# An xLSTM attention and routed feed-forward block: the output combined in expert order instead of in token order

## The chip, the cores and the metric

The kernel runs on one core of one Trainium2 chip. The time is that of the device, in microseconds, of one execution. The kernel before took 240.93 us, the median of 3 runs (239.75 to 241.77).

## The reference, cut to what matters

```python
x = L0_attn_x                          # (16, 256, 128) float32, 4096 tokens
xn = _layernorm(x)
s = _L0_attn_ref(xn, ...)              # 4 heads of 32; each head's row is normalised
                                       # to mean 0 and variance 1, then times (1 + ln_w)
# feed-forward: each token goes to one of 8 experts (argmax of the router)
top1 = argmax(softmax(xn @ router_w + router_b))
for i in range(8):
    a, g = split(xn @ w1[i] + b1[i])   # 128 -> 2 x 512
    y = (a * sigmoid(g)) @ w2[i] + b2[i]
    out = out + where(top1 == i, y, 0)
g = silu(out)
x = x + s * g                          # what is returned
```

So each token's row of the output is its own `x`, plus its attention row `s` times the silu of its expert's row.

## The kernel before, in words

The 4096 tokens are 32 tiles of 128 rows. **First**, up to about 52 us, the rows are normalised and transposed, and the router and gate projections are made; for each token its place in expert order is worked out (`pos`): the tokens of an expert stand together, padded to whole blocks of 128 rows, which makes `NBLK` = 39 blocks in `NCH` = 13 chunks of three. **Then** attention runs over the 16 sequences, up to about 107 us, while POOL scatters the 32 tiles of normalised rows `xw` (each row with its token's number behind it) to `xs_dram` in expert order, with one indirect DMA a tile (line 443). Attention leaves its raw head rows in `u_all`.

**Then** the expert blocks run. In iteration j, PE transposes the rows of block j+1 (`rowsT`, line 1131), makes the hidden products of block j (`hidden`, line 1195: the gate half first, then the other half) and the down products of block j-1 (`down`, line 1204). ACT in iteration j copies the transposed rows out (`evac_xs`, line 606), copies one half of the next block's weights (`copy_w`, line 600), takes the sigmoid of the gate (`gate`, line 612), and the sigmoid for the silu of block j-2 (line 656). DVE copies the other half of the next block's weights (`copy_w`, line 851), multiplies by the gate (`product`, line 976), adds the bias (`add_bias`, line 984) and finishes the silu of block j-2 (`silu`, line 992). PE waits for both weight halves of a block (`s_wc`, `s_wv`), the second half of `hidden` only for DVE's, and `down(j)` waits for `product(j)`. Weights are held three deep, so `copy_w(j+1)` in iteration j waits for `hidden(j-2)`.

Between these pieces DVE does the attention's normalisation in small pieces: `step(normals)` issues the next instruction of the generator `normalise`, three times in an iteration, each after a wait that the one before is done. There are four groups of eight tiles and 25 steps a group: two squares (line 918), two sums (line 920), nineteen small ones on 128x32 elements, and two products with the coefficient (line 934). POOL multiplies each finished group by gamma (line 457) back into `u_all`, between its other work.

POOL scatters each finished silu block to `y_dram` in token order, one indirect DMA a block (line 449); rows that are padding have an index out of bounds and are dropped. SP loads the chunks of sorted rows four deep (line 335), and, after the sixth, reloads `x` (line 341).

**Last**, when all 39 scatters have landed, SP reads `y_dram` back in 8 pieces (line 347); DVE multiplies each piece by the attention rows (line 963); `x` is added by PE in four pieces (lines 1261 and 1265, evacuated by ACT, line 660), by POOL in three (line 465) and by DVE in one (line 968); and SP stores each piece (line 356).

Of the kernel before, what the change touches and what calls it, by code (L numbers as in the profile page):

```python
# [5 lines left out]
F32 = mybir.dt.float32  # L6
# [7 lines left out]
P = 128  # L14


def mlstm_moe_block(nc, x, wq, wk, wv, wi, bi, wf, bf, ln_w, router_w, router_b, w1, b1, w2, b2, out):
# [18 lines left out]
    NX = 4  # L36
# [11 lines left out]
    GROUPS = [(0, 4), (4, 4), (8, 4), (12, 4)]  # L48
    NPC = 8
    TP = T // NPC  # L50
    POOL_PIECES = (2, 4, 6)
    PE_PIECES = (0, 1, 3, 5)
# [4 lines left out]
    GT = 8  # L57
# [7 lines left out]
    y_dram = nc.dram_tensor("y_tokens", (NTOK, D), F32).ap()  # L65
    x_t = x.rearrange("b (k p) d -> p (b k) d", p=P)
    y_t = y_dram.rearrange("(t p) d -> p t d", p=P)
    out_t = out.rearrange("b (k p) d -> p (b k) d", p=P)

    ctx = ExitStack()  # L70
    with ctx:
# [10 lines left out]
        yg = xn  # L82
        xnT = sb("xnT", [P, NTOK])
        u_all = sb("u_all", [P, T, NH, DA])
# [72 lines left out]
        q_all = x_sb[:, :, :].rearrange("p t d -> p (t d)")  # L157

# [12 lines left out]
        sqs = [cflat[:, i * GT * D:(i + 1) * GT * D].rearrange("p (t h d) -> p t h d", t=GT, h=NH) for i in range(2)]  # L171
# [6 lines left out]
        ys_sb = ffn[:, 0:2 * CH * D].rearrange("p (i n d) -> p i n d", i=2, n=CH)  # L178
# [58 lines left out]
        s_yst = [sem(f"s_yst{i}") for i in range(NX)]  # L237
        s_yg = [sem(f"s_yg{i}") for i in range(NPC)]
# [3 lines left out]
        s_fin = sem("s_fin")  # L242
        s_finp = sem("s_finp")
        s_fina = sem("s_fina")
        s_sum = sem("s_sum")
        s_gam = sem("s_gam")
        s_prod = sem("s_prod")
        s_out = sem("s_out")
# [48 lines left out]
        s_xr = sem("s_xr")  # L297
        s_gamma = sem("s_gamma")

        NSMALL = 7  # L300
        block = ctx.enter_context(nc.Block())
# [3 lines left out]
        def _(sp):  # L305
# [22 lines left out]

            sp.wait_ge(s_sub, 5)
            sp.wait_ge(s_scat, 16 * T)  # L330
            for c in range(NCH):
                if c >= NX:
                    sp.wait_ge(s_xsp, (c - NX + 1) * CH)
                    sp.wait_ge(s_idx, c - NX + 1)
                sp.dma_start(xs_sb[:, c % NX, :, :],
                             xs_dram[c * CH * P:(c + 1) * CH * P, :].rearrange("(n p) d -> p n d", p=P)).then_inc(s_xs[c % NX], 16)
                if c == NX + 1:
# [10 lines left out]
            for g in range(NPC):  # L348
                ts = slice(g * TP, (g + 1) * TP)
                if g in POOL_PIECES:  # L350
                    sp.wait_ge(s_finp, POOL_PIECES.index(g) + 1)
                elif g in PE_PIECES:
                    sp.wait_ge(s_fina, PE_PIECES.index(g) + 1)
                else:
                    sp.wait_ge(s_fin, len([i for i in range(g + 1) if i not in POOL_PIECES + PE_PIECES]))
                sp.dma_start(out_t[:, ts, :], yg[:, ts, :]).then_inc(s_out, 16)
            sp.wait_ge(s_out, 16 * NPC)
# [3 lines left out]
        def _(pool):  # L361
# [84 lines left out]
            for j in range(NBLK):  # L446
                pool.wait_ge(s_ye, j + 1)
                pool.wait_ge(s_idx, j // CH + 1)
                pool.indirect_dma_start(y_dram, bass.IndirectOffsetOnAxis(ap=idx[:, j:j + 1], axis=0),  # L449
                    ys_sb[:, j // CH % 2, j % CH, :], None, bounds_check=NTOK - 1, oob_is_err=False).then_inc(s_yst[j // CH % NX], 16)  # L450

                if j in GAMMA_AT:
                    g = GAMMA_AT.index(j)
                    b0, nb = GROUPS[g]
                    pool.wait_ge(s_norm, NSTEPS * (g + 1))
                    pool.wait_ge(s_gamma, 1)
                    pool.tensor_tensor(u_all[:, 2 * b0:2 * (b0 + nb), :, 0:DH], sqs[g % 2],
                                       gamma[:, :].rearrange("p (h d) -> p h d", h=NH).unsqueeze(1).to_broadcast([P, GT, NH, DH]),
                                       ALU.mult).then_inc(s_gam, 1)

            for g in POOL_PIECES:
                y = yg[:, g * TP:(g + 1) * TP, :]
                pool.wait_ge(s_xr, 16 * NPC)
                pool.wait_ge(s_prod, g + 1)
                pool.tensor_tensor(y, y, x_sb[:, g * TP:(g + 1) * TP, :], ALU.add).then_inc(s_finp, 1)
# [3 lines left out]
        def _(act):  # L469
# [187 lines left out]

            for i, g in enumerate(PE_PIECES):
                act.wait_ge(s_sum, i + 1)
# [629 lines left out]
```

## Time and profile before

| | |
|---|---|
| median of 3 runs | 240.93 us (239.75 to 241.77) |
| the profiled execution, its own time | 240.99 us |
| its span in the profile | 239.2 us |
| mean granted TensorE clock | 0.975 |
| PE busy | 209.1 us (87%) |
| DVE busy | 181.8 us (76%) |
| ACT busy | 136.5 us (57%) |
| POOL busy | 100.0 us (42%) |
| moved by DMA | 29.30 MB |

The shares of busy time are averages over stages that have different limits; where the time goes is read from the chain of work that ended last and from the order in time of single instructions. The device time is 1.8 us more than the span of this execution.

### The profile page before, as it was taken

Reading aid. Unit: us, or ns where it says so; the run is one execution under the profiler, and the core shown is the slowest. Engines: PE = TensorE matmul, PEld = TensorE weight load, DVE = VectorE, ACT = ScalarE, POOL = GpSimd, SP = SyncE. Lnnn points to the kernel's source line nnn. Section 1 sums busy time; section 2 is a strip of 40 time slices with the busy share of each in tenths; the row PEclk is TensorE's granted clock in tenths of the full one; section 3 lists DMA queues with packets and bytes.
Section 4 is the critical chain, followed back from the end, with each engine's and each line's share of the span. In section 5 each row is a group of like instructions: output and inputs, shape, how many; then the busy total and the mean of one; then the engine's idle time right before and its main releaser. Section 6 shows DMA issues by size and latency. Waiting matters only on the chain.

```text
span 239.2 us, 6066 instructions
## 1 busy us (share of the span) xinstructions
PE 209.1 (87%) x1824; PEld 170.8 (71%) x1832; DVE 181.8 (76%) x505; ACT 136.5 (57%) x313; POOL 100.0 (42%) x128
## 2 busy tenths in 40 slices
PE   0688879689999999979999999999999999999650
PEld 0568744335555555559999999999999999986310
DVE  6997378299989986648777988898889789671490
ACT  0276756779788796754555555555555655540110
POOL 7553200027777776000333364425533464366150
PEclk9988999999999999999999999999999999999975
DMA  6999999501441111401097021102101000000994
GB/s 175 266 419 418 282 299 394 221 3 46 146 137 53 49 53 59 115 21 33 15 261 204 26 58 52 55 22 62 44 30 50 28 25 25 26 11 13 251 315 137
DMA packets 29730, 29.30 MB, mean 122 GB/s; under 512 B 3295, under 2 KB 24807, under 8 KB 29697
## 3 DMA queue, kind: packets, MB, share of 16 engines
q1 hardware_dynamic: 26258, 24.59, 33.0%
q0 software_dynamic: 2272, 4.22, 5.4%
q8 instruction: 16, 0.26, 0.5%
q10 hardware_dynamic: 1168, 0.10, 0.4%
q14 instruction: 16, 0.13, 0.2%
HBM read 20.01 MB, written 9.34 MB: 123 GB/s over the span
## 4 chain that ended last, share of the span: by engine, by line
PE 67%; DVE 11%; issue 6%; ACT 5%; DMA 5%; DVEq 1%; SPq 1%; POOL 1%; ACTq 0%; POOLq 0%
PE bank L1195 13%; PE head_bank L1195 13%; PE bank L1204 12%; PE head_bank L1159 5%; PE bank L1169 5%; PE bank L1149 4%; PE head_bank L1052 4%; PE bank L1180 3%; PE bank L1148 3%; DMA xw<-y_tokens 2%; DVE stats L696 2%; PE bank L1037 2%; PE bank L1082 2%; DVE cm L859 2%; PE head_bank L1131 1%
## 5 line engine op out<-in xcount | busy, mean ns | idle before, releaser
L449 POOL DMA_INDIRECT y_tokens<-ffn,idx x39 | 39.2, 1004 | 76.3 <-DVE ffn L992 74.0
L443 POOL DMA_INDIRECT xs_sorted<-xw,pos x32 | 33.0, 1031 | 36.3 <-DVE pos L831 26.9
L1204 PE MATMUL bank<-w_sb,dm 128*128 x312 | 41.3, 275 | 0.5 <-DVE dm L976 0.5
L1195 PE MATMUL bank<-xsT,wc 128*128 128x128 f32 x320 | 39.3, 276 | 0.1
L1204 PEld LDWEIGHTS bank<-w_sb,dm 128*128 128x128 f32 x312 | 38.0, 192 | 0.7 <-issue 0.7
L1195 PEld LDWEIGHTS bank<-xsT,wc 128*128 128x128 f32 x320 | 37.4, 192 | 0.5 <-DVE wc L851 0.3
L1195 PE MATMUL head_bank<-xsT,wc 128*128 128x128 f32 x304 | 37.0, 275 | 0.0
L1195 PEld LDWEIGHTS head_bank<-xsT,wc 128*128 128x128 f32 x304 | 35.4, 192 | 0.0
L859 DVE TENSOR_TENSOR cm<-dm,head_bank 128x1024 f32<-128x1024 f32 (+1 forms) x32 | 29.0, 948 | 6.3 <-ACT dm L586 3.5
L600 ACT ACTIVATE wc<-w_sb 128x512 f32 x39 | 24.6, 630 | 14.3 <-issue 14.3
L586 ACT ACTIVATE dm<-bank 128x512 f32<-128x512 f32 x48 | 26.9, 594 | 4.5 <-PE bank L1149 3.5
L606 ACT ACTIVATE xsT<-head_bank 127x128 f32<-127x128 f32 x38 | 10.5, 277 | 27.8 <-PE head_bank L1131 27.8
L851 DVE COPY wc<-w_sb 128x512 f32 x39 | 16.6, 425 | 10.3 <-issue 9.0
L1149 PE MATMUL bank<-right,left 128*128 128x512 bf16 x48 | 15.7, 379 | 2.6 <-ACT x_sb L535 1.0
L1159 PEld LDWEIGHTS head_bank<-x_sb,xnT 32*128 32x128 f32 x256 | 11.7, 184 | 8.0 <-issue 7.7
L976 DVE TENSOR_TENSOR dm<-bank,dm 128x512 f32<-128x512 f32 x20 | 13.6, 681 | 3.7 <-ACT dm L612 2.0
L1159 PE MATMUL head_bank<-x_sb,xnT 32*128 32x256 f32 (+1 forms) x256 | 15.0, 347 | 0.5 <-DVE cm L859 0.4
L976 DVE TENSOR_TENSOR dm<-head_bank,dm 128x512 f32<-128x512 f32 x19 | 13.0, 684 | 2.3 <-ACT dm L612 2.3
L984 DVE TENSOR_TENSOR ffn<-bank,b_sb 128x128 f32<-128x128 f32 x39 | 11.2, 287 | 4.4 <-PE bank L1204 2.1
L656 ACT ACTIVATE ffn<-ffn 128x128 f32<-128x128 f32 x39 | 11.8, 302 | 4.9 <-DVE ffn L984 4.9
L1169 PE MATMUL bank<-cm,u_all 128*32 128x256 f32 (+1 forms) x256 | 13.7, 332 | 0.0
L612 ACT ACTIVATE dm<-bank 128x512 f32<-128x512 f32 x20 | 11.6, 581 | 2.9 <-PE bank L1195 2.9
(199 smaller groups left out, 352.0 us busy)
## 6 DMA issues: line engine op xcount, KB each, us to landing
x_sb<-in_L_attn_x SPq DMA_DIRECT2D x16, 256.0 KB, 5.1
w_sb<-in_L_ffn_w SPq DMA_DIRECT2D x8, 512.0 KB, 8.2
wc<-in_L_ffn_w SPq DMA_DIRECT2D x5, 512.0 KB, 17.1
xs_sb<-xs_sorted SPq DMA_DIRECT2D x13, 193.5 KB, 2.8
xs_sorted<-b_sb SPq DMA_DIRECT2D x1, 2048.0 KB, 17.3
xw<-y_tokens SPq DMA_DIRECT2D x8, 256.0 KB, 4.6
out_x<-xw SPq DMA_DIRECT2D x8, 256.0 KB, 3.6
y_tokens<-ffn,idx POOLq DMA_INDIRECT x39, 2.3
```

The lines of the kernel that those rows point to most:

```text
L443: pool.indirect_dma_start(xs_dram, bass.IndirectOffsetOnAxis(ap=pos[:, t:t + 1], axis=0), xw[:, t, :], None).then_inc(s_scat, 16)
L449: pool.indirect_dma_start(y_dram, bass.IndirectOffsetOnAxis(ap=idx[:, j:j + 1], axis=0), ys_sb[:, j // CH % 2, j % CH, :], None, bounds_ch ...
L586: act.activation(dm[:, b % 2, :, m, :], bank[(3 * b + m) % 2][:, :].rearrange("p (h t) -> p h t", h=NH), ACT.Exp).then_inc(s_dm, 1)
L600: act.activation(wc[:, j % 3, HID:H2], w1_sb[:, bass.ds(e, 1), HID:H2], ACT.Copy).then_inc(s_wc, 1)
L851: dve.tensor_copy(wc[:, j % 3, 0:HID], w1_sb[:, bass.ds(e, 1), 0:HID]).then_inc(s_wv, 1)
L859: dve.tensor_tensor(cm[:, b % 2, :, m0:m1, :], dm[:, b % 2, :, m0:m1, :], head_bank[:, :, m0 * P:m1 * P].rearrange("p h (m t) -> p h m t", ...
L976: dve.tensor_tensor(uT[:, j % 2, :, :].rearrange(flat), bank[2 * (j % 2)][:, :], sg[:, j % 2, :, :].rearrange(flat), ALU.mult).then_inc(s_ ...
L1149: pe.matmul(bank[n % 2][:, :], left[:, b % 4, s0:s0 + P], right[:, :, j, t0:t0 + P], start=(m == 1), stop=True).then_inc(s_ld, 1)
L1159: last = pe.matmul(head_bank[:, h, 2 * k * P:(2 + k) * P], xnT[hs, b * S + k * P:b * S + (k + 1) * P], q_all[hs, b * S + k * P:(b + 1) * S ...
L1169: last = pe.matmul(bank[6][h * DH:(h + 1) * DH, k * P:S], u_all[:, 2 * b + k, h, 0:DH], cm[:, b % 2, h, 2 * k:2 + k, :].rearrange("p m t - ...
L1195: last = pe.matmul(bank[2 * (j % 2) + k][:, c * P:(c + 1) * P], wc[:, j % 3, m:m + P], xsT[:, j % 2, :], start=True, stop=True)
L1204: last = pe.matmul(bank[6 + j % 2][:, 0:D], uT[:, j % 2, c, :], w2_sb[:, bass.ds(e * (HC * D) + c * D, D)], start=(c == 0), stop=(c == HC ...
```

## The change

`y_dram`, the read back in token order and the whole last stage are taken out. In their place the attention rows are brought into expert order, and the combination is made there.

- The normalisation has two groups of sixteen tiles, each in four quarters of 128x512 elements. The squares are made by ACT (`squares(i)`, in iterations 0 to 7, between `evac_xs` and `copy_w`); the result goes into `sall`, which lies in the place of `xnT`. The sums wait for them (`s_sq`). The gamma of the first group is multiplied by POOL in two instructions of 128x1024, after steps 25 and 27; that of the second group by DVE, after each quarter.
- POOL scatters the 32 tiles of finished attention rows into `ss_dram` in expert order, the first sixteen from `hidden(9)` on, the other sixteen from `hidden(18)` on. SP fills `ss_dram` with zeros and copies `x` to the output, DRAM to DRAM, both right after its load of chunk 3. After its load of chunk 10, SP waits for all 32 scatters and loads ten chunks of `ss`; the other three follow as slots come free.
- The silu blocks stay in `yall`, ten chunks deep, in the place of `xw`. `combine(c)` multiplies a whole chunk (128x384) by its `ss` rows, in iterations 27 to 38 for chunks 0 to 11; the three blocks of chunk 12 are multiplied singly in `silu`.
- POOL then scatters the 39 blocks to the output rows with an adding indirect DMA (`compute_op=ALU.add`), the first when `combine(0)` is done. The kernel ends when these have landed.

```diff
-    GROUPS = [(0, 4), (4, 4), (8, 4), (12, 4)]
-    NSTEPS = 25
-    GAMMA_AT = (9, 18, 27, 34)
+    GROUPS = [(0, 8), (8, 8)]
+    NQ = 4
+    SMALL_STEPS = NQ + 19
+    NSTEPS = (SMALL_STEPS + NQ, SMALL_STEPS + 2 * NQ)
+    NSLOT = 10
+    COMBINE_AT = [27 + c for c in range(NCH - 1)]
...
@@ SP @@
+                if c == NX - 1:
+                    blanks = zeros[:, :]
+                    sp.dma_start(ss_of_p[:, 0:full * S].rearrange("p (n c) -> p n c", n=full),
+                                 blanks.unsqueeze(1).to_broadcast([P, full, S])).then_inc(s_ssf, 16)
+                    sp.dma_start(ss_of_p[:, full * S:NBLK * D], blanks[:, 0:NBLK * D - full * S]).then_inc(s_ssf, 16)
+                    sp.dma_start(out_rows, x.rearrange("b s d -> (b s) d")).then_inc(s_pre, 16)
+                if c == NCH - 3:
+                    sp.wait_ge(s_ss, 16 * T)
                     sp.wait_ge(s_sc, B)
-                    for g in range(NPC):
-                        ts = slice(g * TP, (g + 1) * TP)
-                        sp.dma_start(x_sb[:, ts, :], x_t[:, ts, :]).then_inc(s_xr, 16)
-            for i in range(NX):
-                sp.wait_ge(s_yst[i], 16 * CH * len(range(i, NCH, NX)))
-            for g in range(NPC):
-                ts = slice(g * TP, (g + 1) * TP)
-                sp.dma_start(yg[:, ts, :], y_t[:, ts, :]).then_inc(s_yg[g], 16)
...
+                    for i in range(NSLOT):
+                        load_s(i)
+            for i in range(NSLOT, NCH):
+                sp.wait_ge(s_cb, i - NSLOT + 1)
+                load_s(i)
@@ POOL @@
-            for j in range(NBLK):
-                pool.wait_ge(s_ye, j + 1)
-                pool.wait_ge(s_idx, j // CH + 1)
-                pool.indirect_dma_start(y_dram, bass.IndirectOffsetOnAxis(ap=idx[:, j:j + 1], axis=0),
-                    ys_sb[:, j // CH % 2, j % CH, :], None, bounds_check=NTOK - 1, oob_is_err=False).then_inc(s_yst[j // CH % NX], 16)
...
+            def scatter_s(t):
+                pool.indirect_dma_start(ss_dram, bass.IndirectOffsetOnAxis(ap=pos[:, t:t + 1], axis=0),
+                                        sall[:, t, :, :].rearrange("p h d -> p (h d)"), None).then_inc(s_ss, 16)
+            pool.wait_ge(s_gamma, 1)
+            for i in range(2):
+                rows = sall[:, i * 2 * QT:(i + 1) * 2 * QT, :, :]
+                pool.wait_ge(s_norm, SMALL_STEPS + 2 * (i + 1))
+                pool.tensor_tensor(rows, rows, gamma_hd(2 * QT), ALU.mult).then_inc(s_gam, 1)
+            pool.wait_ge(s_ssf, 32)
+            for t in range(GT):
+                pool.wait_ge(s_gam, t // (2 * QT) + 1)
+                pool.wait_ge(s_h, 10 + t // 2)
+                scatter_s(t)
+            for t in range(GT, T):
+                pool.wait_ge(s_norm, NSTEPS[0] + SMALL_STEPS + 2 * ((t - GT) // QT + 1))
+                pool.wait_ge(s_h, 19 + (t - GT) // 3)
+                scatter_s(t)
+            pool.wait_ge(s_pre, 16)
+            for c in range(NCH):
+                for n in range(CH):
+                    j = CH * c + n
+                    if c < NCH - 1:
+                        pool.wait_ge(s_cb, c + 1)
+                    else:
+                        pool.wait_ge(s_ye, j + 1)
+                    pool.wait_ge(s_idx, c + 1)
+                    pool.indirect_dma_start(out_rows, bass.IndirectOffsetOnAxis(ap=idx[:, j:j + 1], axis=0),
+                                            yall[:, c % NSLOT, n, :], None, bounds_check=NTOK - 1, oob_is_err=False,
+                                            compute_op=ALU.add).then_inc(s_ost[min(c, NCH - NSLOT)], 16)
@@ ACT @@
+            def squares(i):
+                ts = slice(i * QT, (i + 1) * QT)
+                act.wait_ge(s_sc, B)
+                act.wait_ge(s_oe, (i + 1) * QT // 2)
+                act.activation(sall[:, ts, :, :], u_all[:, ts, :, 0:DH], ACT.Square).then_inc(s_sq, 1)
             for j in range(NBLK + 2):
                 if j + 1 < NBLK:
                     evac_xs(j + 1)
+                if j < 2 * NQ:
+                    squares(j)
                 if 1 <= j < NBLK - 1:
                     copy_w(j + 1)
@@ DVE @@
+                for i, (a, b) in enumerate(quarters):
+                    dve.wait_ge(s_sq, NQ * g + i + 1)
+                    yield dve.tensor_reduce(ssum[:, a * NH:b * NH], sall[:, t0 + a:t0 + b, :, :], AX.X, ALU.add)
...
+                for a, b in quarters:
+                    rows = sall[:, t0 + a:t0 + b, :, :]
+                    yield dve.tensor_tensor(rows, uv[:, a:b, :, :],
                                             coef[:, a * NH:b * NH].rearrange("p (t h) -> p t h", h=NH).unsqueeze(3).to_broadcast([P, b - a, NH, DH]),
                                             ALU.mult)
+                    if g == 1:
+                        dve.wait_ge(s_gamma, 1)
+                        yield dve.tensor_tensor(rows, rows, gamma_hd(QT), ALU.mult)
...
+            def combine(c):
+                y = yall[:, c % NSLOT, :, :]
+                dve.wait_ge(s_ye, CH * (c + 1))
+                dve.wait_ge(s_ssl[c], 16)
+                dve.tensor_tensor(y, y, ss[:, c % NSLOT, :, :], ALU.mult).then_inc(s_cb, 1)
...
                 if j >= 2:
                     silu(j - 2)
+                if j in COMBINE_AT:
+                    combine(COMBINE_AT.index(j))
                 step(normals)
-            while step(normals):
-                pass
-            finish()
```

The last stage's instructions on PE, ACT and POOL go with `finish()`.

## Rows read from the trace of the kernel before

**Rows 1.** The page, busy time by engine: busy us, share, instructions.
```profile
PE 209.1 (87%) x1824; PEld 170.8 (71%) x1832; DVE 181.8 (76%) x505; ACT 136.5 (57%) x313; POOL 100.0 (42%) x128
```
**Rows 2.** Chain of work that ended last: start us, us, engine, tile, line.
```profile
211.69 1.80 PE bank L1195 x16
...
217.60 0.98 POOL y_tokens L449
218.89 2.10 DMA y_tokens<-ffn,idx
```
**Rows 3.** Order in time, PE: start us, us, line, operation [idle before].
```profile
110.86 1.95 PE L1195 MATMUL bank<-xsT,wc 128*128 128x128 f32 x16
...
135.96 1.95 PE L1195 MATMUL head_bank<-xsT,wc 128*128 128x128 f32 x16
...
144.33 2.31 PE L1195 MATMUL bank<-xsT,wc 128*128 128x128 f32 x16
...
180.95 1.95 PE L1195 MATMUL head_bank<-xsT,wc 128*128 128x128 f32 x16
...
211.52 1.95 PE L1195 MATMUL bank<-xsT,wc 128*128 128x128 f32 x16
```
**Rows 4.** Order in time, POOL.
```profile
91.30 0.96 POOL L443 DMA_INDIRECT xs_sorted<-xw,pos  x1 [0.31 <-issue]
92.56 0.96 POOL L443 DMA_INDIRECT xs_sorted<-xw,pos  x1 [0.30 <-issue]
...
141.77 2.39 POOL L457 TENSOR_TENSOR u_all<-cm,gamma 128x1024 f32<-128x1024 f32 x1
...
186.02 0.98 POOL L449 DMA_INDIRECT y_tokens<-ffn,idx  x1 [1.25 <-DVE ffn L992]
...
217.60 0.98 POOL L449 DMA_INDIRECT y_tokens<-ffn,idx  x1 [0.30 <-issue]
218.89 0.98 POOL L449 DMA_INDIRECT y_tokens<-ffn,idx  x1 [0.31 <-issue]
```
**Rows 5.** Line 449's instructions: duration ns min/median/max, and the way to landing.
```profile
L449 POOL DMA_INDIRECT y_tokens<-ffn,idx x39: 982/984/1147, 115.1 to 218.9; - x39
DMA to landing us min/median/max: 2.1/2.3/4.3
```
**Rows 6.** Order in time, DVE.
```profile
112.20 0.43 DVE L851 COPY wc<-w_sb 128x512 f32 x1
...
131.85 0.42 DVE L851 COPY wc<-w_sb 128x512 f32 x1
132.19 0.68 DVE L918 TENSOR_TENSOR cm<-u_all 128x512 f32<-128x512 f32 x1
...
134.98 0.41 DVE L851 COPY wc<-w_sb 128x512 f32 x1
...
141.54 2.68 DVE L930 TENSOR_SCALAR veps<-ssum 128x32 f32<-128x32 f32 x1
...
184.97 0.28 DVE L992 TENSOR_TENSOR ffn<-ffn 128x128 f32<-128x128 f32 x1
```
**Rows 7.** Order in time, ACT, the row copy of iteration 3.
```profile
113.85 0.28 ACT L606 ACTIVATE xsT<-head_bank 127x128 f32<-127x128 f32 x1 [0.82 <-PE head_bank L1131]
```
**Rows 8.** Groups of instructions by line, keeping shapes apart: busy us, mean ns | idle before.
```profile
L600 ACT ACTIVATE wc<-w_sb 128x512 f32 x39 | 24.6, 630 | 14.3 <-issue 14.3
L920 DVE TENSOR_REDUCE ssum<-cm 128x16 f32<-128x512 f32 x8 | 5.4, 675 | 0.0
```
**Rows 9.** SP's queue in order of time, and the page's issues with us to landing.
```profile
119.81 6.14 SPq L341 DMA_DIRECT2D x_sb<-in_L_attn_x  x8
x_sb<-in_L_attn_x SPq DMA_DIRECT2D x16, 256.0 KB, 5.1
xs_sb<-xs_sorted SPq DMA_DIRECT2D x13, 193.5 KB, 2.8
```
**Rows 10.** Stretch with one scatter an iteration: us, busy (x) of PE, PEld, DVE, ACT, POOL, PEclk, DMA share, GB/s.
```profile
186.00:213.00 27.00, 27.00 (x245) 27.00 (x244) 21.20 (x60) 14.93 (x37) 14.08 (x12) 1.00 0.07 24
```

More of the change, by code:

```diff
@@ L64, in mlstm_moe_block @@
     xs_dram = nc.dram_tensor("xs_sorted", (NBLK * P, DW), F32).ap()
-    y_dram = nc.dram_tensor("y_tokens", (NTOK, D), F32).ap()
+    ss_dram = nc.dram_tensor("s_sorted", (NBLK * P, D), F32).ap()
     x_t = x.rearrange("b (k p) d -> p (b k) d", p=P)
-    y_t = y_dram.rearrange("(t p) d -> p t d", p=P)
-    out_t = out.rearrange("b (k p) d -> p (b k) d", p=P)
+    out_rows = out.rearrange("b s d -> (b s) d")
     ctx = ExitStack()
@@ L236, in mlstm_moe_block @@
         s_ye = sem("s_ye")
-        s_yst = [sem(f"s_yst{i}") for i in range(NX)]
-        s_yg = [sem(f"s_yg{i}") for i in range(NPC)]
+        s_ssl = [sem(f"s_ssl{c}") for c in range(NCH)]
+        s_ost = [sem(f"s_ost{i}") for i in range(NCH - NSLOT + 1)]
+        s_ss = sem("s_ss")
+        s_ssf = sem("s_ssf")
+        s_pre = sem("s_pre")
+        s_cb = sem("s_cb")
+        s_sq = sem("s_sq")
+        s_mix = sem("s_mix")
         s_norm = sem("s_norm")
@@ L296, in mlstm_moe_block, with gamma_hd @@
         s_xone = sem("s_xone")
-        s_xr = sem("s_xr")
         s_gamma = sem("s_gamma")
         NSMALL = 7
+        def gamma_hd(n):
+            return gamma[:, :].rearrange("p (h d) -> p h d", h=NH).unsqueeze(1).to_broadcast([P, n, NH, DH])
         block = ctx.enter_context(nc.Block())
@@ L336, in _ @@
                              xs_dram[c * CH * P:(c + 1) * CH * P, :].rearrange("(n p) d -> p n d", p=P)).then_inc(s_xs[c % NX], 16)
-                if c == NX + 1:
-                    sp.wait_ge(s_sc, B)
-                    for g in range(NPC):
-                        ts = slice(g * TP, (g + 1) * TP)
-                        sp.dma_start(x_sb[:, ts, :], x_t[:, ts, :]).then_inc(s_xr, 16)
-            for i in range(NX):
-                sp.wait_ge(s_yst[i], 16 * CH * len(range(i, NCH, NX)))
-            for g in range(NPC):
-                ts = slice(g * TP, (g + 1) * TP)
-                sp.dma_start(yg[:, ts, :], y_t[:, ts, :]).then_inc(s_yg[g], 16)
[L348 to L357, printed above, removed]
+                if c == NX - 1:
[6 more added lines that the diff above has]
+                    sp.wait_ge(s_ss, 16 * T)
+                    sp.wait_ge(s_sc, B)
+                    for i in range(NSLOT):
[3 more added lines that the diff above has]
+                load_s(i)
+            for i in range(NCH - NSLOT + 1):
+                sp.wait_ge(s_ost[i], 16 * CH * (1 if i < NCH - NSLOT else NSLOT))
         @block.gpsimd
@@ L656, in _ @@
                     act.activation(sy[:, j % 2, :], yb[:, j % 2, :], ACT.Sigmoid).then_inc(s_sy, 1)
-            for i, g in enumerate(PE_PIECES):
-                act.wait_ge(s_sum, i + 1)
-                act.activation(yg[:, g * TP:(g + 1) * TP, :], bank[i][:, :].rearrange("p (t d) -> p t d", d=D), ACT.Copy).then_inc(s_fina, 1)
         @block.vector
@@ L911, in normalise @@
                 dve.wait_ge(s_oe, b0 + nb)
[L912 to L920 removed]
+                t0 = 2 * b0
+                quarters = [(i * nt // NQ, (i + 1) * nt // NQ) for i in range(NQ)]
+                for i, (a, b) in enumerate(quarters):
+                    dve.wait_ge(s_sq, NQ * g + i + 1)
+                    yield dve.tensor_reduce(ssum[:, a * NH:b * NH], sall[:, t0 + a:t0 + b, :, :], AX.X, ALU.add)
+                yield dve.scalar_tensor_tensor(den[:, 0:n].rearrange("p (t h) -> p t h", h=NH), rs, -1.0, rs, ALU.mult, ALU.max)
                 d4 = den[:, 0:n].rearrange("p (b k h) -> p b k h", k=2, h=NH)
[L923 removed]
                 yield dve.tensor_tensor(d4, d4, tm[:, :, :].rearrange("p k (h b) -> p b k h", h=NH)[:, b0:b0 + nb, :, :], ALU.max)
@@ L953, in _ @@
             norms = [0]
-            def finish():
-                for g in range(NPC):
-                    ts = slice(g * TP, (g + 1) * TP)
-                    y = yg[:, ts, :]
-                    hd = "p t (h d) -> p t h d"
-                    dve.wait_ge(s_yg[g], 16)
-                    dve.wait_ge(s_gam, len(GROUPS))
-                    dve.tensor_tensor(y.rearrange(hd, h=NH), y.rearrange(hd, h=NH), u_all[:, ts, :, 0:DH],
-                                      ALU.mult).then_inc(s_prod, 1)
-                    if g not in POOL_PIECES + PE_PIECES:
-                        dve.wait_ge(s_prod, g + 1)
-                        dve.wait_ge(s_xr, 16 * NPC)
-                        dve.tensor_tensor(y, y, x_sb[:, ts, :], ALU.add).then_inc(s_fin, 1)
             def product(j):
```

75 lines of the change are left out of this document (24 added, 51 removed).

## The prediction, made before the result was known

> **What bounds the kernel now.** I read the page's busy shares first, to see that no engine fills the span: PE is at 87%, POOL at 42% [rows 1]. Then the chain of waits. From about 108 us on it is one PE link after another up to the last hidden products at 211.69; then come POOL's last scatters and a landing of 2.10 from 218.89 [rows 2]; behind it stand the read back, the last products and the stores. Then PE in order of time: hidden(2) starts at 110.86 and hidden(38) at 211.52, 36 iterations at 2.80 us [rows 3]. Only once in that stretch is a hidden longer than 1.95 (2.31, at 144.33), so PE sets the pace, and DVE, ACT and POOL are late by less than PE forgives. The last stage, from the landing at 221.0 to the end at 239.2, is 18.2 us. This is what the change takes out; the question is what is then last.
>
> **The queue of adding scatters.** Before, POOL had one scatter an iteration, started about 0.77 us after its silu, as the one of block 25: silu from 184.97 to 185.25 [rows 6], scatter at 186.02 [rows 4]. After, all 39 output scatters stand behind combine(0), which DVE makes in iteration 27, right behind silu(25), and they stand in one queue. Back to back, POOL starts a scatter every 1.29 us at the end of the kernel and every 1.26 beside attention: 0.96 to 0.98 busy and 0.30 of issue each [rows 4]. Three a chunk are 3.9 us, where chunks come every 2.80. So POOL falls behind from the first chunk, and the end is that of a queue:
> - combine(0), 128x384 with both inputs in SBUF, lies between 0.28 for 128x128 and 0.68 for 128x512 [rows 6]; 0.55 by interpolation. It ends at 185.7, and the first adding scatter starts at 186.5.
> - 38 intervals. Their ends: 1.26, and 1.45, which is the longest scatter seen, 1.147, plus 0.30 [rows 4, 5]. I take 1.30, since the median is 0.984 and some beside a busy DVE are longer: 49.4 us, last start at 235.9.
> - Landing 2.1 to 4.3, median 2.3 [rows 5]: 238.2, and 0.1 to the span's end: **238.3**.
>
> That stands against a span of 239.2. Of the 18.2 us removed 17.3 come back as a queue on POOL, before any delay upstream. No row shows a scatter that adds. From below I give it the plain price (nothing in the trace excludes that it costs no more), from above the longest duration and the longest landing: 38 x 0.15 + 2.0 = 7.7 us more. The nearest row is the plain scatter to DRAM of the same 128 rows, so I take its price and keep the upper end for the range.
>
> **What delays iteration 27.** The chain starts at a fixed iteration, so each microsecond that PE or DVE loses before it moves the end by one.
> - *Squares on ACT, sums on DVE.* Each square is 128x512 from SBUF to SBUF, as the weight copy at 0.63; ACT, at 57%, has room for eight. But DVE's steps outrun them. The third step of iteration 1 is the sum of quarter 3, and its square stands on ACT behind the row copy of iteration 3, which ends at 114.13 [rows 7]. Square to 114.8, sum (0.675, [rows 8]) to 115.4, 0.3 of issue, then copy_w(3) to 116.1, which before ended at 112.63 [rows 6]. hidden(3) starts at 113.66 (110.86 + 2.80) and wants it for its second half at 114.6. PE loses **1.5 us**; bounds 0 and 2.
> - *Gamma on POOL.* Before, DVE's step of 128x32 at 141.54 took 2.68 us, ending with POOL's 128x1024 product (141.77, 2.39): DVE's instruction was held [rows 4, 6]. Before, such products were eight iterations apart and PE lost 0.4 at the worst. After, there are two, after steps 25 and 27, in iterations 8 and 9, where DVE is fullest: it goes from copy at 131.85 to copy at 134.98 without a gap, 3.13 us for a pace of 2.80 [rows 6]. Two holds are 3.8 to 4.8 us; copy_w(11) has 1.5 us to spare (ends 135.39, wanted at 136.86, 0.9 after 135.96). That leaves 2.3 to 3.3; less the 0.4 lost before, and some of a hold falling on the sums, I take **2.2**; bounds 0 and 4.
>
> The Trainium skill (SBUF — State Buffer, Who interferes with whom) says that the port pair is held for the whole instruction by whoever issues first, and that `tensor_reduce` never contends. By that rule the four sums of group 1 next to the products run on, and copies and two-input products wait; the trace agrees as far as it goes (2.68 beside 2.39). If sums were held as well, the stall would be nearer the upper bound, 4.
>
> - *DVE, the rest.* Removed: eight squares and eight products become twelve others of like size, so the number of heavy steps hardly falls; the second group's eight products in iterations 17 to 19 go at 3.13 an iteration, 1.0 us late over three, inside the 1.5 to spare. The twelve combines meet iterations without steps. Nothing.
> - *POOL before the queue.* 32 scatters of attention rows. The first sixteen start at about 141 and end by 161; the others start with hidden(18) done, at about 161, and 16 x 1.26 = 20.2 bring them to 182, landed by 185. SP then issues ten loads, 2.8 us to landing [rows 9]: chunk 0 is there at about 189, when combine(0) comes at 185.7 + 3.7 = 189.4. Hidden, but by little. If it failed, it would cost 1 to 3 us. Loads of chunks 11 and 12 wait behind this on SP, and are wanted only four iterations later.
> - *SP after chunk 3.* The fill (2.5 MB) and the copy of x (2 MB read and written) go ahead of chunk 4. Eight loads of 256 KB were issued in 6.14 and landed 5.1 later, 2 MB in 11 us [rows 9]. So the fill is 14 and the copy 11 to 22: from 99.5, done by 125 to 136; chunk 4 is wanted in iteration 11, at about 137. Hidden, with 1 us at the worst. Taken out: the reload of x and the read back; the former cost PE nothing.
>
> **Sum.** 238.3 + 1.5 + 2.2 = 242.0 span. The profiled execution was 240.99 for 239.2, 1.8 more, and 0.06 above the median: **243.8 us**. A difference of 1% (238.5 to 243.3) is about what a measurement of this kernel can tell from none.
>
> **Rivals.**
> - *The queue as computed, PE's stalls forgiven.* DVE's lateness has been absorbed nearly wholly in the trace (one hidden at 2.31 against four gamma products). Against: never two holds in two iterations, never a step that waits for ACT. Time: 238.3 to 239.8 and 1.8, **240.1 to 241.6**, no change. 20%.
> - *An adding scatter is dearer than a plain one*, in POOL's work or because its landing holds the next. Each 0.1 us an interval is 3.8. At 1.45 and a landing of 4.3, with the stalls, **251.5**, or more. For: every row must be read, added to and written back. Against: with a plain scatter every 2.8 us the DMA engines are busy 0.07 of the time [rows 10], and POOL need not wait for a landing. 13%.
> - *Faster: the intervals are shorter than 1.29.* The place is the 0.30 of issue between scatters. Without it 38 x 0.30 = 11.4 are saved: span 230.6 with the stalls, **232.4**. With stalls, 238.5 is passed only below 1.16 an interval (5.3 us over 38); without stalls at 1.26, the rate beside attention. For: the new waits are met long before, so that nothing has to come in from another engine. Against: 0.30 to 0.31 before every back-to-back scatter [rows 4]. 8%.
> - The Trainium skill (SBUF — State Buffer, the trap of DVE blocking a DMA) has POOL locked out of writing descriptors while DVE copies from SBUF to SBUF, 0.62 us growing to 3.1. As a mechanism of this kernel it would be one hold for each of the eleven copies beside the queue. The rows show scatters beside such copies at 1.147 at most, so 11 x 0.16 = 1.8 us, **245.6**; it lies inside the case I forecast, a third of whose chance it has.
>
> **How the numbers follow.** The forecast case, queue and stalls, has 59% and spans 241.5 to 249. The range leaves out the rest of the fast rival and half of the dear one: 239.5 to 251. Slower by over 1% (above 243.3): two thirds of 59% and the 13%, 0.53. Within 1%: a third of 59% and 18% of the second, 0.38. Faster: 0.09.
>
> **What would show it.** Right: POOL issues 39 scatters to the output without a gap, 1.3 us apart, from about 190 to 240, with PE idle after 218; hidden(3) is some 3.4 us long; a copy or product of DVE beside each POOL product is 2 us or more; hidden(27) starts about 3.7 us later than at 180.95 [rows 3]. Wrong: intervals above 1.4; hidden(27) before 182; a combine that waits for a load; scatters that wait for DVE, which would mean that POOL keeps up.

## The result, and the profile after

The changed kernel takes **273.66 us** (median of 4 runs, 272.50 to 274.71) against 240.80 us for the one before, measured beside it: 1.1365 times, with a 95% interval of 1.1295 to 1.1434. I had forecast 243.8 in a range of 239.5 to 251.0: the sign was right, the size far off. The profiled execution took 272.50 us for a span of 270.6.

The page of the changed kernel, its busy times, the row of the software queue (packets, MB, share) and its POOL groups (line 477 is the output scatter, line 447 that of the normalised rows, line 451 that of the attention rows; line 458, further down, is POOL's product with gamma):

```profile
span 270.6 us, 6060 instructions
PE 198.2 (73%) x1798; PEld 164.3 (61%) x1798; DVE 172.0 (64%) x469; ACT 137.9 (51%) x317; POOL 145.7 (54%) x155
...
q0 software_dynamic: 7664, 6.32, 13.3%
...
L477 POOL DMA_INDIRECT out_x<-xw,idx x39 | 61.6, 1579 | 18.1 <-issue 10.4
L447 POOL DMA_INDIRECT xs_sorted<-xw,pos x32 | 33.0, 1030 | 36.4 <-DVE pos L849 26.9
...
L451 POOL DMA_INDIRECT s_sorted<-xnT,pos x32 | 32.0, 1000 | 11.8 <-issue 7.5
```

POOL's busy time grew from 100.0 to 145.7 us [rows 1], and not by number alone: the two plain kinds of scatter take 1.00 and 1.03 us, the adding one 1.58. The chain of waits names it too: from 209 us on it is one POOL link behind another. Here are POOL in order of time at the start of the queue and at its end, and then the summary of line 477 and line 70, where the program closes (EVENT_SEMAPHORE and DRAIN are the sequencers' own; for them too the columns are ns and start):

```profile
182.61 0.96 POOL L451 DMA_INDIRECT s_sorted<-xnT,pos  x1 [0.30 <-issue]
190.04 1.61 POOL L477 DMA_INDIRECT out_x<-xw,idx  x1 [6.47 <-DVE xw L1008]
191.96 1.58 POOL L477 DMA_INDIRECT out_x<-xw,idx  x1 [0.30 <-issue]
...
261.65 1.55 POOL L477 DMA_INDIRECT out_x<-xw,idx  x1 [0.30 <-issue]
```
```profile
L477 POOL DMA_INDIRECT out_x<-xw,idx x39: 1554/1554/1926, 190.0 to 261.7; - x39
...
L70 POOLq DRAIN  x1: 29477/29477/29477, 240.9 to 240.9; - x1
...
L70 SPq COMPARE_BRANCH  x1: 37/37/37, 264.5 to 264.5; - x1
...
L70 SPq EVENT_SEMAPHORE  x1: 17/17/17, 270.6 to 270.6; - x1
```

Three things are to be seen. The queue is there from 190.04 to 261.65 with nothing but 0.30 us between two scatters, which the view calls issue (the engine waits for nothing that the profile shows): 38 intervals in 71.61 us, **1.884 us** each, where plain scatters stood 1.29 apart [rows 4]. Its start is where I put it (190.2). And the program does not end with the last landing: SP is past its waits at 264.5, but POOL's closing DRAIN runs until 240.91 + 29.48 = 270.4, and the closing events of the other engines stand behind it. (The DRAIN is entered at 240.91, when twelve scatters are still to start, so its length says little; what counts is its end, 7.2 us behind the end of the last scatter.)

On PE the two losses upstream can be read directly. PE in order of time, the iterations around them, and hidden(27):

```profile
107.65 1.95 PE L1210 MATMUL head_bank<-xsT,wc 128*128 128x128 f32 x16
...
113.23 1.06 PE L1210 MATMUL head_bank<-xsT,wc 128*128 128x128 f32 x8
115.57 1.16 PE L1210 MATMUL head_bank<-xsT,wc 128*128 128x128 f32 x8 [1.28 <-DVE wc L869]
...
117.56 1.95 PE L1210 MATMUL bank<-xsT,wc 128*128 128x128 f32 x16
...
136.91 1.15 PE L1219 MATMUL bank<-w_sb,dm 128*128 x8 [0.66 <-DVE dm L978]
...
138.01 1.06 PE L1210 MATMUL head_bank<-xsT,wc 128*128 128x128 f32 x8
140.93 1.16 PE L1210 MATMUL head_bank<-xsT,wc 128*128 128x128 f32 x8 [1.86 <-DVE wc L869]
...
185.18 1.95 PE L1210 MATMUL head_bank<-xsT,wc 128*128 128x128 f32 x16
```

The second half of hidden(3) waits 1.28 us for DVE's weight copy, down(9) 0.66 for its product, and the second half of hidden(11) 1.86 for the copy again. What a wait costs is read from the starts, since it is more than the idle time shown: hidden(4) starts 4.33 us behind hidden(3) (117.56 and 113.23), 1.54 over the pace of 2.79; hidden(12) at 143.30 starts 9.00 behind hidden(10) at 134.30, 3.42 over two iterations. DVE in order of time shows why: first the sums that wait for squares (line 934, behind ACT's line 663), then two instructions of 2.86 and 2.45 us. The last two lines are POOL's, its two products with gamma beside them:

```profile
111.54 0.69 DVE L934 TENSOR_REDUCE ssum<-xnT 128x16 f32<-128x512 f32 x1 [1.12 <-ACT xnT L663]
...
114.33 0.69 DVE L934 TENSOR_REDUCE ssum<-xnT 128x16 f32<-128x512 f32 x1 [1.68 <-ACT xnT L663]
115.09 0.43 DVE L869 COPY wc<-w_sb 128x512 f32 x1
...
132.97 0.42 DVE L869 COPY wc<-w_sb 128x512 f32 x1
133.31 2.86 DVE L948 TENSOR_TENSOR xnT<-u_all,coef 128x512 f32<-128x512 f32 x1
...
137.49 2.45 DVE L996 TENSOR_TENSOR xw<-ffn 128x128 f32<-128x128 f32 x1
139.87 0.67 DVE L934 TENSOR_REDUCE ssum<-xnT 128x16 f32<-128x512 f32 x1
```
```profile
133.21 2.41 POOL L458 TENSOR_TENSOR xnT<-xnT,gamma 128x1024 f32<-128x1024 f32 x1 [39.06 <-DVE xnT L948]
137.44 2.35 POOL L458 TENSOR_TENSOR xnT<-xnT,gamma 128x1024 f32<-128x1024 f32 x1 [1.83 <-DVE xnT L948]
```

The runs differ by up to 4 us in when the expert blocks begin (hidden(1) at 107.65 to 111.56; e8 apart), so below I compare from the start of hidden(1) on. In the changed kernel that is 107.65, hidden(27) comes **77.53 us** behind it, the queue 4.86 behind that, and the end 162.95 behind hidden(1). Before: hidden(1) at 108.07, hidden(27) at 180.95 [rows 3], 72.88 behind.

### The profile page after: what moved, and what is told of

Read it like the earlier page. It is cut to its first block, busy times and chain, and to the rows that moved or that the text cites. A ratio compares the mean times of both kernels' runs of the same rounds, so it can differ in the third digit from the quotient of the medians.

```text
span 270.6 us, 6060 instructions
## 1 busy us (share of the span) xinstructions
PE 198.2 (73%) x1798; PEld 164.3 (61%) x1798; DVE 172.0 (64%) x469; ACT 137.9 (51%) x317; POOL 145.7 (54%) x155
## 3 DMA queue, kind: packets, MB, share of 16 engines
q0 software_dynamic: 7664, 6.32, 13.3%
## 4 chain that ended last, share of the span: by engine, by line
PE 57%; POOL 16%; DVE 9%; issue 6%; ACT 4%; DMA 2%; POOLq 1%; ACTq 1%; DVEq 1%; SPq 1%
POOL out_x L477 16%; PE bank L1210 11%; PE head_bank L1210 11%; PE bank L1219 10%; PE head_bank L1174 4%; PE bank L1184 4%; PE bank L1163 3%; PE bank L1164 3%; PE bank L1195 3%; PE head_bank L1067 2%; DMA x_sb<-in_L_attn_x 2%; PE bank L1097 2%; DVE stats L714 1%; DVE cm L877 1%; PE head_bank L1146 1%
## 5 line engine op out<-in xcount | busy, mean ns | idle before, releaser
L477 POOL DMA_INDIRECT out_x<-xw,idx x39 | 61.6, 1579 | 18.1 <-issue 10.4
L1210 PE MATMUL head_bank<-xsT,wc 128*128 128x128 f32 x304 | 37.6, 276 | 3.1 <-DVE wc L869 3.1
L451 POOL DMA_INDIRECT s_sorted<-xnT,pos x32 | 32.0, 1000 | 11.8 <-issue 7.5
L600 ACT ACTIVATE dm<-bank 128x512 f32<-128x512 f32 x48 | 26.9, 594 | 4.6 <-PE bank L1164 3.5
L458 POOL TENSOR_TENSOR xnT<-xnT,gamma 128x1024 f32<-128x1024 f32 x2 | 4.8, 2378 | 40.9 <-DVE xnT L948 40.9
L869 DVE COPY wc<-w_sb 128x512 f32 x39 | 17.8, 457 | 8.3 <-issue 7.1
```

The lines of the kernel that those rows point to most:

```text
L451: pool.indirect_dma_start(ss_dram, bass.IndirectOffsetOnAxis(ap=pos[:, t:t + 1], axis=0), sall[:, t, :, :].rearrange("p h d -> p (h d)"), ...
L477: pool.indirect_dma_start(out_rows, bass.IndirectOffsetOnAxis(ap=idx[:, j:j + 1], axis=0), yall[:, c % NSLOT, n, :], None, bounds_check=NT ...
L600: act.activation(dm[:, b % 2, :, m, :], bank[(3 * b + m) % 2][:, :].rearrange("p (h t) -> p h t", h=NH), ACT.Exp).then_inc(s_dm, 1)
L869: dve.tensor_copy(wc[:, j % 3, 0:HID], w1_sb[:, bass.ds(e, 1), 0:HID]).then_inc(s_wv, 1)
L1210: last = pe.matmul(bank[2 * (j % 2) + k][:, c * P:(c + 1) * P], wc[:, j % 3, m:m + P], xsT[:, j % 2, :], start=True, stop=True)
```

## The experiments

My theory after the result was that **the adding mode** makes POOL's own part of a scatter dearer (A). The rival was **the place**: the output tensor as target, the tile in the place of `xw` as source, or the queue (B). For the last 6 us: the closing drain takes its time behind whatever POOL did last (C), or it belongs to adding (D).

**e1_plain.** The same kernel without the addition.

```diff
-                                            yall[:, c % NSLOT, n, :], None, bounds_check=NTOK - 1, oob_is_err=False,
-                                            compute_op=ALU.add).then_inc(s_ost[min(c, NCH - NSLOT)], 16)
+                                            yall[:, c % NSLOT, n, :], None, bounds_check=NTOK - 1, oob_is_err=False).then_inc(s_ost[min(c, NCH - NSLOT)], 16)
```

> The changed kernel with its 39 output scatters as plain writes (the addition of x to the output is left out). Theory A, the adding mode itself makes POOL's part of a scatter dearer: each of the 39 takes 0.98 us instead of 1.55, one starts every 1.29 to 1.31 us, from 190.0 to a last start at 239.4. Theory B, it is the place (the output tensor, the source tile, the queue itself): 1.55 us stays, last start near 261. For the end: theory C, POOL's closing drain takes some 7 us behind its last scatter whatever its kind: span 247.6, 249.5 us. Theory D, the 6 us between the last landing and the end come from adding: span 241.9, 243.8 us.

Measured: 255.39 us, 1.060 times the kernel before (1.046 to 1.075), span 253.2. The group of line 477 and, from the same page, the software queue; then POOL's last two scatters in order of time, and POOL's row of the closing line:

```profile
L477 POOL DMA_INDIRECT out_x<-xw,idx x39 | 39.6, 1015 | 16.8 <-issue 10.4
...
q0 software_dynamic: 3296, 6.32, 7.2%
```
```profile
242.24 0.98 POOL L477 DMA_INDIRECT out_x<-xw,idx  x1 [0.30 <-issue]
243.52 0.98 POOL L477 DMA_INDIRECT out_x<-xw,idx  x1 [0.30 <-issue]
```
```profile
L70 POOLq DRAIN  x1: 23930/23930/23930, 229.1 to 229.1; - x1
```

From the same tile to the same rows, a plain scatter takes 0.98 us and stands 1.32 from the next on average (193.3 to 243.52). So it is the mode: A holds, B falls. The drain ends at 253.0, 8.5 us behind the last scatter's end: it does not belong to adding, which speaks for C, though the distance is 1.3 longer than behind an adding scatter, and why is not shown. (The 247.6 expected became 253.2: hidden(1) at 110.92 is 3.3 later, 0.8 more lie in the intervals and 1.3 in the drain.) The queue row tells more: the same bytes (6.32 MB) go out in 3296 packets instead of 7664, that is (7664 - 3296) / 39 = 112 packets fewer a scatter of 128 rows. And even if adding cost nothing the change would have been slower than the kernel before.

**e2_before_add.** The other way round: the kernel before, its scatters made adding ones where they stood.

```diff
                 pool.indirect_dma_start(y_dram, ...,
-                    ys_sb[:, j // CH % 2, j % CH, :], None, bounds_check=NTOK - 1, oob_is_err=False)
+                    ys_sb[:, j // CH % 2, j % CH, :], None, bounds_check=NTOK - 1, oob_is_err=False,
+                    compute_op=ALU.add)
...
+                if c == NX - 1:
+                    sp.dma_start(y_dram (as 128 x 4096), zeros repeated).then_inc(s_yz, 16)
...
+            pool.wait_ge(s_yz, 16)
```

> The kernel before, with its 39 scatters into y_tokens as adding scatters (and y_tokens filled with zeros first, by one more DMA behind the load of chunk 3). Theory A: each takes 1.55 us, and one an iteration of 2.80 us hides that; only the last four, back to back, cost 3 x 0.56 = 1.7 and 0.4 to 1 more in landing: span 241.3, 243.1 us. Theory B: 0.98 us as before and no change, 240.9 us. A third, that an adding scatter also slows the engines or transfers beside it, would show as hidden products longer than 1.95 us and over 245 us.

Measured: 248.38 us, 1.031 times (1.022 to 1.041), span 247.1. Line 454's group in this kernel:

```profile
L454 POOL DMA_INDIRECT y_tokens<-ffn,idx x39 | 61.4, 1574 | 60.5 <-DVE ffn L998 59.1 <-issue 1.4
...
L463 POOL TENSOR_TENSOR u_all<-cm,gamma 128x1024 f32<-128x1024 f32 x4 | 11.8, 2944 | 0.0
```

A again: 1.57 us, now in the old place, and mostly one by one, 2.3 us or more apart; so the price is not that of a scatter queued behind the one before it. The blocks do hide it: from hidden(1) to hidden(38) PE needs 104.98 us against 103.45. The time is 5 us over what I expected, though, and over the 245 that the third theory named. But the hidden products in the blocks keep their 1.95 us, so that theory's other sign is absent. Of the 7.9 us of span, 1.5 are in those blocks, where each of POOL's four gamma products now covers 2.94 us instead of 2.39 and PE waits 0.64, 0.19 and 0.27 for DVE's copy; 3.0 lie behind hidden(38), where I had expected 2.1 to 2.7 (the last scatter starts 2.3 later, since the last four stand behind a longer gamma product too, and the rest follows 0.7 later); and 3.3 lie ahead of hidden(1), of which 1.55 is hidden(0), 3.57 us long instead of 2.02, at a lower granted clock. The other 1.8 are a later start of hidden(0), which also differs by 2.3 us among kernels with the same code ahead of it (103.67 in the changed kernel, 106.00 in e5); why is not shown.

**e5_half_rows.** What POOL's price depends on: adding rows half as long.

```diff
-                    pool.indirect_dma_start(out_rows, bass.IndirectOffsetOnAxis(ap=idx[:, j:j + 1], axis=0),
-                                            yall[:, c % NSLOT, n, :], None, ...
+                    pool.indirect_dma_start(out.rearrange("b s (k d) -> (b s k) d", k=2), bass.IndirectOffsetOnAxis(ap=idx[:, j:j + 1], axis=0),
+                                            yall[:, c % NSLOT, n, 0:64], None, ...
```

> The changed kernel, its 39 adding scatters with rows of 64 elements instead of 128 (half of each row is left out, and the rows go to other places of the output). If POOL's work is set by the number of rows, each still takes 1.55 us and the span is as before, 270.6 or 1.5 less. If it is set by the bytes, each takes between 0.98 and 1.27 us, and the last starts near 250.

Measured: 275.29 us, span 274.5. The summary of its line 477, its software queue, and its count of packets:

```profile
L477 POOL DMA_INDIRECT out_x<-xw,idx x39: 1554/1554/1932, 194.1 to 265.6; - x39
```
```profile
DMA packets 30288, 31.24 MB, mean 114 GB/s; under 512 B 8585, under 2 KB 25361, under 8 KB 30225
...
q0 software_dynamic: 7664, 5.27, 11.0%
```

The median is 1.554 us to the nanosecond, first and last start are 71.5 us apart, and there are the same 7664 packets, with half the bytes in each row. So POOL's price does not go with the bytes. Rows or instructions it cannot tell, since every scatter here has 128 indices; the packets, 144 against 32, differ with the mode as the price does. The span is 3.9 us over the expected one because hidden(1) comes at 111.56, 3.9 later; from there to the end it is 162.94 us, against 162.95.

**e3_no_pool_gamma.** The holds of DVE taken away.

```diff
-                pool.tensor_tensor(rows, rows, gamma_hd(2 * QT), ALU.mult).then_inc(s_gam, 1)
+                pool.tensor_tensor(rows[:, 0:1, 0:1, 0:1], rows[:, 0:1, 0:1, 0:1], gamma_hd(1)[:, :, 0:1, 0:1], ALU.mult).then_inc(s_gam, 1)
```

> The changed kernel with POOL's two products with gamma cut to one element (gamma is left out for the first group). If the two holds of DVE (2.86 and 2.45 us) cost PE its 2.5 us of waits at hidden(10) and hidden(11), hidden(27) starts at 182.7 instead of 185.2, the queue of output scatters at 187.5, and span and time fall by 2.5 us (span 268.1). If DVE's fullness alone did it, hidden(27) moves by less than 1 us.

Measured: 270.67 us, span 269.2. Hidden(1) at 109.65, hidden(27) at 183.72: 74.07 us, 3.46 less than in the changed kernel where I expected 2.5 (I had summed the idle times shown, 0.66 and 1.86, and not the starts), and hidden(1) to the end is 159.55 against 162.95, 3.4 less. The same stretch of DVE as above:

```profile
135.31 0.68 DVE L948 TENSOR_TENSOR xnT<-u_all,coef 128x512 f32<-128x512 f32 x1
135.92 0.68 DVE L978 TENSOR_TENSOR dm<-head_bank,dm 128x512 f32<-128x512 f32 x1
...
137.12 0.28 DVE L986 TENSOR_TENSOR ffn<-bank,b_sb 128x128 f32<-128x128 f32 x1
137.32 0.29 DVE L996 TENSOR_TENSOR xw<-ffn 128x128 f32<-128x128 f32 x1
```

The product that took 2.86 us takes 0.68 and the silu 0.29 instead of 2.45. DVE is as full as before and PE does not wait at hidden(10) and hidden(11): it was the holds. All of it arrives at the end.

**e4_squares_early.** The wait for the squares taken away.

```diff
-                if j < 2 * NQ:
-                    squares(j)
+                for i in {0: (0, 1, 2, 3), 2: (4,), 3: (5,), 4: (6,), 5: (7,)}.get(j, ()):
+                    squares(i)
```

> The changed kernel with ACT's first four squares all in iteration 0 and the other four in iterations 2 to 5. If the wait of PE in hidden(3) (1.3 us) is the sum on DVE that waits for a square behind ACT's later row copy, that wait goes, hidden(27) starts at 183.9, and the end falls by 1.3 us (span 269.3). If four squares in a row hold ACT so that PE waits for its weight copy in iteration 1 or 2 instead, nothing is gained.

Measured: 274.13 us, span 273.0, which looks like nothing gained. In the trace hidden(3) is whole again, 1.95 us at 115.98:

```profile
115.98 1.95 PE L1210 MATMUL head_bank<-xsT,wc 128*128 128x128 f32 x16
...
118.77 1.95 PE L1210 MATMUL bank<-xsT,wc 128*128 128x128 f32 x16
```

hidden(4) starts 2.79 behind it, so the 1.54 us are gone. But the span holds two stretches in which the granted clock was at its lower level for a part. These are windows of PE, in this kernel over hidden(0), in this kernel over the second half of hidden(11), and in the changed kernel over its own (us, busy (x), granted clock, DMA share, GB/s); 1.00 is the upper level, and inside the first of them, from 105 to 107, it is 0.50:

```profile
104.00:109.00 5.00, 4.41 (x34) 0.66 1.08 382
```
```profile
141.50:147.50 6.00, 5.38 (x33) 0.72 0.26 77
```
```profile
140.00:146.00 6.00, 4.95 (x41) 1.00 0.26 77
```

Hidden(1) to hidden(27) is 77.18 us. A run of the unchanged changed kernel that had the same dip at hidden(11) (e9, below) needs 78.74, so 1.56 were gained, beside 0.35 against the run without it. (The span is 273.0 and not the 269.3 expected because hidden(1) is at 110.40, 2.75 later, and the second dip costs 1.2.) The wait was the squares; its 1.54 us are about what a dip of the clock costs, and the times alone would not have shown it.

**e6_before_pool_024 and e7_before_pool_02.** The closing drain, on the kernel before: POOL's last work moved forward.

```diff
-    POOL_PIECES = (2, 4, 6)
-    PE_PIECES = (0, 1, 3, 5)
+    POOL_PIECES = (0, 2, 4)            # e7: (0, 2)
+    PE_PIECES = (1, 3, 5, 6)           # e7: (1, 3, 4, 5, 6), keep_warm on bank 5
```

> The kernel before, with POOL adding x to pieces 0, 2 and 4 of the last stage and PE to 1, 3, 5 and 6, so that POOL's last product ends some 2.8 us earlier (230.3 instead of 233.1). Theory C, POOL's closing drain ends some 6 us behind its last instruction whatever that is: the drain ends at 236.3 instead of 239.05, and the end is then that of the stores, landed at 238.0: span 238.3, a gain of 0.9 us. Theory D, the drain waits for something else that ends near the stores' landing: span 239.2, no change.

> The kernel before, with POOL adding x to pieces 0 and 2 only and PE to 1, 3, 4, 5 and 6. Theory C: the drain ends near 233.5, and the stores alone set the end: span 238.0 to 238.5. Theory D: the drain still ends about a microsecond behind the stores' landing, 239.2. A rival to both: PE, whose clock is low in this stage, is late with five pieces, and the stores land later than 238.0.

Measured: e6 239.98 us, 0.9969 times (0.9933 to 1.0005), not told from no change, though its profiled span is the 238.3 expected; e7 239.27 us, **0.9937** times (0.9905 to 0.9970), in 12 runs against 23 of the kernel before. The drain's rows, of the kernel before, of e6 and of e7:

```profile
L71 POOLq DRAIN  x1: 7422/7422/7422, 231.6 to 231.6; - x1
...
L71 SPq EVENT_SEMAPHORE  x1: 17/17/17, 239.2 to 239.2; - x1
```
```profile
L71 POOLq DRAIN  x1: 7547/7547/7547, 229.6 to 229.6; - x1
```
```profile
L71 POOLq DRAIN  x1: 7100/7100/7100, 226.8 to 226.8; - x1
```

POOL's last product ends at 233.12, 231.23 and 227.98; the drains end at 239.04, 237.15 and 233.9: 5.92 us behind it, three times. C holds. In the kernel before SP was past its wait for the stores at 238.2 and the drain ended at 239.04, 0.15 us ahead of the span's end; so there too POOL's drain ended last, by 0.8 us. e7 takes POOL out of it and is the fastest of all kernels here, by little. Its profiled execution is the slowest of its 12 (span 239.3, over the 238.0 to 238.5 expected); SP passed the stores only at 239.1 there, and they set the end. So its gain rests on the runs, and as e7 also moves work from POOL to PE, how much of it is the drain's is not shown.

**e8_queue_earlier, e9_after_again, e10_queue_earlier_again.** The start of the queue moved.

```diff
-    COMBINE_AT = [27 + c for c in range(NCH - 1)]
+    COMBINE_AT = [25 + c for c in range(NCH - 2)] + [38]
...
+                pool.wait_ge(s_ssf, 32)
+                pool.wait_ge(s_gam, i + 1)
+                for t in range(2 * QT * i, 2 * QT * (i + 1)):
+                    scatter_s(t)
-            pool.wait_ge(s_ssf, 32)
-            for t in range(GT):
-                pool.wait_ge(s_gam, t // (2 * QT) + 1)
-                pool.wait_ge(s_h, 10 + t // 2)
-                scatter_s(t)
...
-                pool.wait_ge(s_h, 19 + (t - GT) // 3)
```

> The changed kernel with the combines of chunks 0 to 10 two iterations earlier (25 to 35), and with POOL's scatters of attention rows released as soon as their rows are ready (the first eight between the two products with gamma, no wait for hidden products). If the end is the start of the queue plus 39 intervals, the start moves by two iterations, 5.6 us, and so does the end: hidden(1) to the end is 157.4 instead of 163.0 us, span about 265 to 267. If POOL's scatters are ready no sooner, or the loads behind them come late, combine(0) waits, DVE with it, and PE shows it as a longer iteration 25 or 26; the end then moves by less. Either way it stays slower than the kernel before, since POOL's own work behind iteration 9 is 32 x 1.26 + 39 x 1.86 = 113 us.

> The changed kernel again, beside the next one on the same chip, since the first run of that one met a chip on which even the kernel before took 253.8 us. Every theory: hidden(27) 77.5 us behind hidden(1), the queue 4.9 us behind that, 71.6 us to its last start, and 8.9 us from there to the end.

> As for e8_queue_earlier, which this repeats: if the end is the start of the queue plus 39 scatters, the queue starts two iterations (5.6 us) earlier behind hidden(1) than in e9_after_again, and the span is 5.6 us shorter. If combine(0) waits for its attention rows instead, DVE waits in iteration 25, a hidden product follows late on PE, and the gain is smaller or turns into a loss.

e8 (307.75 us) says nothing of the start of the queue: it ran on a chip on which the kernel before took 253.82 us, and in its trace PE nearly stands still from 204 to 211 us with no releaser that the profile shows. Its queue runs from 225.9 to 297.4 and the span ends at 306.3, 80.4 us behind the queue's start. Side by side on an ordinary chip, e9 takes 274.14 and e10 271.57 us. The queue's start is 83.65 us behind hidden(1) in e9 and 80.34 in e10, and the end 164.15 and 160.84: 3.31 us less at both. The two queues, e9 first, and then DVE in e10 at combine(0), which now meets an attention chunk that has not landed:

```profile
L477 POOL DMA_INDIRECT out_x<-xw,idx x39: 1554/1555/1930, 193.1 to 264.7; - x39
```
```profile
L475 POOL DMA_INDIRECT out_x<-xw,idx x39: 1552/1552/1945, 189.2 to 260.7; - x39
```
```profile
187.73 0.56 DVE L1006 TENSOR_TENSOR xw<-xw,x_sb 128x384 f32<-128x384 f32 x1 [3.75 <-DMA x_sb<-s_sorted]
```

That wait of 3.75 us takes back most of the two iterations (5.58). And the 3.31 are not all theirs: hidden(25) comes 71.52 us behind hidden(1) in e10 and 73.17 in e9, 1.65 sooner. e9 has a dip of the clock at hidden(11) that e10 has not, and in e10 the two gamma products stand further apart. So this schedule cannot start the queue much earlier. What the pair does show is that the end keeps the distance: from the queue's start to the end it is 80.4 to 80.6 us in all seven runs with the 39 adding scatters at the end (after, e3, e4, e5, e8, e9, e10). The queue's start, POOL's 39 scatters and its closing drain set the end.

## Why the prediction was wrong

**The mechanism was right.** A queue on POOL that starts at iteration 27, has no gap and outlasts PE by far (PE ends at 219.9, the queue's last start is at 261.65) is what I forecast, and e3 and e10 show that the end follows its start one to one.

**The term that failed is the price of an adding scatter.** I took 1.30 us an interval, that of the plain one, "since nothing in the trace excludes that it costs no more", and let the longest plain scatter with its issue, 1.45, stand for the upper end. It is 1.884: 38 x 0.58 = **22.2 us**. No row bounded it, and an upper end made from rows of another operation is no bound. I had named this as a rival and given it 13%, with a price per interval (3.8 us for each 0.1) that was right; multiplied by 38, so open a price deserved a far wider range. My argument against it, that the DMA engines had time to spare [rows 10], was true and beside the point: their share is 0.36 in the queue, but the price is POOL's own time for the instruction, 1.55 us instead of 0.98 (e1), whatever the bytes (e5).

**The step that was missing is the closing drain.** I added 0.1 us from the last landing to the end. It is 6.2, since POOL closes 7.2 us behind its last scatter. It could have been suspected from the trace of before: the drain ended at 239.04 in a span of 239.2. I followed the chain of waits, which does not go through its end. Together with 0.4 more of landing (2.7 instead of 2.3): **6.5 us**. Nor was the price everything: e1, with scatters at the plain price, still takes 255.39 us, over my range, and its end lies 9.7 us behind the last start where I had 2.4 (3.3 more are a late start of its blocks).

The rest held. Queue start: 190.04 against 190.2 (-0.2), so close by some luck, as said under gamma. Sum: 22.2 + 6.5 - 0.2 = 28.5, and 270.6 - 242.0 = 28.6.

- *Squares*: PE lost 1.54 where I took 1.5, at hidden(3), by the path given: a sum that waits for its square (1.68 us idle at 114.33), and the weight copy behind it. Confirmed by e4, where hidden(4) follows hidden(3) at the pace again.
- *Gamma on POOL*: two holds, 2.86 and 2.45 us; they cost 3.46 where I took 2.2, inside 0 to 4. hidden(27) came 77.53 instead of 72.88 behind hidden(1), 4.65 later where I had 3.7. The queue's start still fitted because this run's blocks began 0.4 us earlier and the queue followed hidden(27) 0.7 sooner than I had it. Both instructions held are products of two tiles in SBUF, which agrees with the rule of the Trainium skill cited in the prediction (SBUF — State Buffer, Who interferes with whom). The further part of that rule, that sums run on and copies wait, has no test here: the sum at 139.87 starts when POOL's product (137.44 + 2.35 = 139.79) is over, and no copy was held.
- *SP behind chunk 3*: the fill landed 9.5 us behind its issue and the copy of `x` 10.7; no load of rows was late. *Loads behind the attention scatters*: ready in time at iteration 27, 3.75 us late at 25 (e10), so the cover was thin, as I had said.
- *The rival "faster"*: no interval was shorter than 1.85; the issue of 0.30 is there in every one.
- *DVE's copies starving POOL*: scatters beside a busy DVE took up to 1.93 us instead of 1.55 (line 477's summary), the first 17 of the queue 1.61 on average by their rows. That is 0.9 us in all, half of the 1.8 I gave it; that it is DVE's copies which do it is not shown.

## What to carry to other kernels

Before work is moved into a single queue, ask for the price of one item under its new mode, and multiply: an unknown price that stands 39 times in a row needs a measurement by itself, or a range to match. The kernel before hid 35 of its 39 scatters, one an iteration; gathered behind a barrier at iteration 27 the same scatters need 50 us plain and 72 adding, more than the whole last stage (18 us) that they replace. And look at where each engine's closing drain ends: in these kernels POOL's last work would have to end 6 us (a product) to 8.5 us (a plain scatter) before that of the others.

## What the runs showed that I had not expected

- An indirect scatter that adds takes POOL 1.554 us for 128 rows, whether they have 128 or 64 elements; a plain one takes 0.98 (with 128). The adding one lands 3.3 us (median) behind its issue against 2.4. It goes out in 144 packets where a plain one has 32: e1's 3296 are 103 plain scatters of 32, and (7664 - 64 x 32) / 39 = 144.
- POOL's closing drain ends 5.92 us behind a last product (e2 has it a fourth time, 240.97 to 246.9) and 7.2 (adding) or 8.5 us (plain) behind a last scatter. What it does in that time the trace does not show.
- TensorE's granted clock fell from its upper level (2.4 GHz) to the lower one (1.2 GHz) for about a block in some runs and not in others, at the same places: in hidden(0), ahead of which PE had waited 0.2 to 0.6 us (2.02 us long in the changed kernel, 3.57 to 3.65 in e1, e2, e3, e4 and e5), and behind the wait of 1.86 or 1.87 us in hidden(11) (e4 and e9, not the changed kernel's first profile, e1 or e5). It is worth 1.2 to 1.6 us each time, in kernels that do the same there, so an effect of that size can't be read from one profile unless the clock is read beside it. Why it comes is not shown.
